# A delta-rule attention block with a quantised feed-forward: beta's products in four column groups of the TensorE array, and a new placing of NOPs in PE's stream

## The chip, the cores and the metric

The kernel runs on one core of a Trainium2 chip. Its engines are named as the profile names them: PE (TensorE, with PEld for its weight loads), DVE (VectorE), ACT (ScalarE), POOL (GpSimd) and SP (SyncE, which issues most DMAs). The metric is the time of one execution on the device in microseconds, the median of several runs.

## The reference

Input x has shape [2, 4096, 512]. With xn its layer norm, the output is x + attention(xn) + feed-forward(xn).

```python
q, k = xn @ Wq, xn @ Wk;  v = silu(xn @ Wv)         # 16 heads of 32
q, k = l2n(q) * 32 ** -0.5, l2n(k)                  # per head
beta = sigmoid(xn @ Wb)                             # one number per token and head
# per head, over the 4096 tokens:
#   S_t = S_{t-1} + k_t (beta_t * (v_t - S_{t-1}^T k_t))^T ;  o_t = S_t^T q_t
o = o * rsqrt(mean(o * o) + 1e-5) * o_norm_weight
attention = o @ Wo
feed_forward = ((silu(xn @ f8(gate) * gs) * (xn @ f8(up) * us)) @ f8(down)) * ds   # inner width 1536
```

Wb has 16 columns, one per head, where Wq, Wk and Wv have 512: beta is the smallest of the projections.

## The kernel before, in words

**Spans.** The 4096 tokens are cut into 16 spans of 256 tokens for each of the two batch rows, so a span has TOK = 512 tokens, held as TILES = 4 tiles of 128. All 16 spans are written out in Python (`all_spans`, `for turn in range(TURNS)`), each engine in its own stream with waits on semaphores. The first span is the opening, in which weights are still rounded and scaled. Precision comes from splitting: xn stands in SBUF as `xt_hi` and `xt_lo` (fp16, features on the partitions, 512 tokens along the row), the weights as `w_hi` and `w_lo`; a product of a projection is the sum of hi x hi, hi x lo and lo x hi over 4 slices of 128 features.

**PE in a span.** `project(job)` (L440) makes one block of 128 output columns for all 512 tokens, in 12 products of 128x512, into one of four PSUM banks D. The jobs in order are K0, Q0, K1, Q1, beta, (pair 0), K2, (pair 1), Q2, K3, (pair 2), Q3, first part of V0, (pair 3), the rest of V0 and V1 to V3. A pair, `grams_of(m)` (L465), is the key and query pair of head group m: 64 small fp32 products in tiles of 32x32, each of them two loads and two products in the profile, four tiles at a time (`quads`, L370). It waits for `kwide_ready` and `qwide_ready`, which ACT raises when K and Q of that group are out of PSUM. After the projections come the output projection of the span before (L391, 48 products), 18 "halves" of the gate and up projection (`gate_up`, L455, 8 products of 128x512 each), and then the solve and the chain: 4 groups of solve products and 8 chunk steps, in which PE and DVE alternate and the rest of the feed-forward (`fill`) lies between them.

**Beta before.** Beta is job 4. Its weights take 128 columns of `w_hi` (L120), of which for each of the four head groups 4 hold the high part, 4 the low part, and 24 are zeros. Eight products of 128x512 (L448 with two of the three parts) give D[bank] = [128, 512]. DVE's `b_to_tokens` (L1140) transposes all of it in blocks of 32x32 into `bt` (L1142) and adds high and low part into `tb` (L1147, three instructions, because the second batch row's heads are stored with the halves of the partitions exchanged, `parts_of`). ACT's `beta_tanh` (L684) is one activation on `tb` (L687). DVE's `beta_to_problems` then makes the sigmoid of it.

**DVE and ACT around it.** In every span after the opening DVE runs `prepare`: o_sums, k_to_tokens(0), k_to_tokens(1), o_scale, b_to_tokens, k_to_tokens(2), read_grams(0), mask_products(0), o_low, beta_to_problems and on to the solve, a chain of 62 instructions with others woven in (L1274, L1281). ACT runs evacuate_k(0), evacuate_q(0), evacuate_k(1), evacuate_q(1), evacuate_k(2), the high part of o (L717, released by DVE's o_scale), beta_tanh, evacuate_q(2), evacuate_k(3), evacuate_q(3). In the opening, ACT has squares and magnitudes of weights between the evacuations, with beta_tanh ahead of evacuate_k(2), and DVE does its k_to_tokens(0) to (3) in a row (L1133, twelve instructions).

**Slots.** PE's code arrives in blocks of 256 instructions. `addr_align(256, offset=s, max_nops=n)` pads with NOPs until the next instruction stands in slot s of its block. Before, each span after the opening has one such place, in the gate and up run behind half 8 (L514), with 14 NOPs each time; a span is then 18 blocks of instructions long.

## Time and profile before

| | us |
|---|---|
| median of 3 runs | 2225.53 (2224.4 to 2226.23) |
| the profiled execution | 2224.83 |
| its span in the profile | 2222.9 |
| PE busy | 2103.2 (95%) |
| DVE busy | 1874.2 (84%) |
| ACT busy | 1113.6 (50%) |
| POOL busy | 281.8 (13%) |

The busy time of PE counts a product until its modelled end, so products that follow each other closely overlap in it: a product of 128x512 has 0.38 us, and the next one starts about 0.22 us after it. Start times are therefore the better measure. The share of busy time is a mean over stages: in the chain PE and DVE wait for each other, elsewhere PE runs through.

### The profile page before, as it was taken

What the parts mean: (1) busy time and instruction counts of PE and PEld (TensorE: products, weight loads), DVE (VectorE), ACT (ScalarE), POOL (GpSimd) and SP (SyncE); (2) the same over time, 40 slices, a digit from 0 to 9 for tenths busy, and PEclk for the clock granted to TensorE, in tenths of its full rate; (3) what the DMA queues carried; (4) which work ended last, traced back from release to release, by engine and by line L of the source; (5) the groups of instructions that cost most, each with busy time, mean ns of one, the idle gap of its engine ahead of it and who ended that gap; (6) DMA issues with size and microseconds to landing.
All of it is one profiled execution on the core that took longest, in us unless ns stands there. A gap on an engine that the chain in (4) does not pass through costs nothing.

```text
span 2222.9 us, 82460 instructions
## 1 busy us (share of the span) xinstructions
PE 2103.2 (95%) x36464; PEld 1085.0 (49%) x36592; DVE 1874.2 (84%) x3381; ACT 1113.6 (50%) x2840; POOL 281.8 (13%) x534
## 2 busy tenths in 40 slices
PE   2889999999999999999999999999999999999996
PEld 1445454554445555454554545455454554545453
DVE  8988979888797888979888797888979888797886
ACT  4673644636355363644636355462644637355442
POOL 3101111020110201111020110201111020111100
PEclk9999999999999999999999999999999999999998
DMA  7001111001111001111001111001111001111000
GB/s 270 14 9 22 39 22 40 15 10 39 22 40 22 12 31 22 39 23 39 17 8 40 22 40 22 12 31 22 39 22 40 17 7 40 22 39 22 12 12 21
DMA packets 89953, 68.49 MB, mean 31 GB/s; under 512 B 68480, under 2 KB 68480, under 8 KB 89600
## 3 DMA queue, kind: packets, MB, share of 16 engines
q1 hardware_dynamic: 88880, 63.20, 9.7%
q8 instruction: 289, 4.73, 0.9%
q14 instruction: 64, 0.52, 0.1%
q10 hardware_dynamic: 720, 0.03, 0.0%
HBM read 30.72 MB, written 16.78 MB: 21 GB/s over the span
## 4 chain that ended last, share of the span: by engine, by line
PE 86%; DVE 6%; ACT 4%; issue 3%; DMA 1%; SPq 0%; ACTq 0%; DVEq 0%
PE D L460 27%; PE D L450 23%; PE D L525 13%; PE T L375 12%; PE D L391 8%; PE T L367 4%; DVE state L1388 2%; ACT kpv L752 1%; ACT at L777 1%; ACT f_hi L739 1%; DVE outer_p L1384 1%; DMA qt<-in_L_attn_Wq_dram 1%; DVE outer_v L1274 0%; DVE at L1281 0%; DVE amax L1003 0%
## 5 line engine op out<-in xcount | busy, mean ns | idle before, releaser
L460 PE MATMUL D<-xt,wgu 128*128 128x512 f16 x3072 | 685.8, 380 | 9.8 <-ACT sg L745 6.4
L450 PE MATMUL D<-xt,w_hi 128*128 128x512 f16 x1664 | 489.8, 381 | 24.1 <-DVE w_lo L1046 24.1
L460 PEld LDWEIGHTS D<-xt,wgu 128*128 128x128 f16 x3072 | 292.6, 98 | 360.2 <-ACT sg L745 6.9
L450 PE MATMUL D<-xt,w_lo 128*128 128x512 f16 x768 | 292.3, 381 | 0.0
L525 PE MATMUL D<-wd,f_lo 128*128 128x512 bf16 x704 | 267.3, 380 | 13.0 <-issue 12.0
L833 ACT ACTIVATE qt<-T 64x128 f32<-64x128 f32 (+1 forms) x384 | 104.7, 273 | 347.8 <-DVE outer_p L1384 344.8
L525 PE MATMUL D<-wd,f_hi 128*128 128x512 bf16 x704 | 267.3, 380 | 10.2 <-issue 10.2
L1274 DVE TENSOR_TENSOR outer_v<-mt,at 128x62 f32<-128x62 f32 (+15 forms) x496 | 260.6, 525 | 13.6
L1281 DVE TENSOR_TENSOR at<-at,outer_v 128x62 f32<-128x62 f32 (+15 forms) x496 | 260.3, 525 | 11.8
L450 PEld LDWEIGHTS D<-xt,w_hi 128*128 128x128 f16 x1664 | 159.1, 98 | 213.0 <-issue 26.9
L735 ACT ACTIVATE kpv<-kpv,rk 128x32 f32<-128x32 f32 x1024 | 231.1, 308 | 35.5 <-DVE kpv L1138 35.5
L745 ACT ACTIVATE sg<-D,gs 128x512 f32<-128x512 f32 x192 | 131.4, 685 | 185.1 <-PE D L460 184.2
L949 POOL TENSOR_TENSOR xs<-xs,fuse 128x512 f32<-128x512 f32 x64 | 81.1, 1267 | 777.8 <-DVE fuse L1357 777.8
L729 ACT ACTIVATE sg<-D,w_inv 64x256 f32<-64x256 f32 (+1 forms) x192 | 90.3, 470 | 108.2 <-PE D L450 106.6
L391 PE MATMUL D<-wo_hi,qt 128*128 128x512 f16 x480 | 142.8, 379 | 0.0
L1388 DVE SCALAR_TENSOR_TENSOR state<-outer_p,of_pair,state 128x256 f32<-128x256 f32 x256 | 125.5, 531 | 4.5
L450 PEld LDWEIGHTS D<-xt,w_lo 128*128 128x128 f16 x768 | 75.3, 98 | 91.0 <-issue 1.4
L375 PEld LDWEIGHTS T<-kpv 32*32 32x32 f32 x8192 | 89.9, 103 | 55.8 <-issue 55.0
L367 PEld LDWEIGHTS T<-kq,state 64*64 64x64 f32 x4096 | 76.8, 134 | 76.5 <-issue 76.4
L1296 DVE STREAM_TRANSPOSE kq<-T 128x256 f32<-128x256 f32 x128 | 56.9, 444 | 67.4 <-PE T L375 67.4
L525 PEld LDWEIGHTS D<-wd,f_hi 128*128 128x128 f16 x768 | 74.9, 98 | 75.9 <-issue 3.9
L367 PE MATMUL T<-kq,state 64*64 64x64 f32 x4096 | 92.8, 225 | 19.9 <-DVE state L1388 10.3
(181 smaller groups left out, 2864.5 us busy)
## 6 DMA issues: line engine op xcount, KB each, us to landing
xs<-_attn_hidden_states_dram SPq DMA_DIRECT2D x32, 512.0 KB, 3.4
out_dram<-xs SPq DMA_DIRECT2D x32, 512.0 KB, 2.8
fuse<-in_L_ffn_gate_w_dram SPq DMA_DIRECT2D x2, 768.0 KB, 8.9
xs<-in_L_ffn_up_w_dram SPq DMA_DIRECT2D x2, 768.0 KB, 9.0
f_hi<-in_L_ffn_down_w_dram SPq DMA_DIRECT2D x2, 768.0 KB, 10.5
f_lo<-in_L_ffn_down_w_dram SPq DMA_DIRECT2D x2, 768.0 KB, 12.0
kpv<-in_L_attn_Wk_dram SPq DMA_DIRECT2D x1, 1024.0 KB, 11.4
qt<-in_L_attn_Wq_dram SPq DMA_DIRECT2D x1, 1024.0 KB, 13.6
```

Of the source, the lines that this page charges most:

```text
L367: last = nc.tensor.matmul(out[to], lhs[s], rhs[s], start=True, stop=True)
L375: last = nc.tensor.matmul(out[to], lhs[s], rhs[s], start=True, stop=True)
L391: ins = nc.tensor.matmul(D[bank][:, :], o_part[:, m, j * P:(j + 1) * P], w[:, m, :], start=n == 0, stop=n == 11)
L450: last = nc.tensor.matmul(D[bank][:, :], w[:, k, cols], xp[:, k, :], start=n == 0, stop=n == len(products) - 1)
L460: last = nc.tensor.matmul(D[bank][:, :], wgu[:, n // 2, c:c + P], (xt_hi, xt_lo)[n % 2][:, n // 2, :], start=n == 0, stop=n == 2 * KT_ - 1)
L525: last = nc.tensor.matmul(D[bank][:, :], (f_hi, f_lo)[n % 2][:, ic, j * P:(j + 1) * P], wd[:, ic, :], start=n == 0, stop=n == 2 * IC - 1)
L735: return nc.scalar.activation(v_problem, v_problem, ACT.Identity, scale=rk[:, n:n + 1])
L745: nc.scalar.activation(sg[:, ic % 2, :], D[bank_of(gate_up_job(2 * ic))][:, :], ACT.Silu, scale=gs[:, ic:ic + 1]).then_inc(sg_ready, 1)
L833: last = nc.scalar.activation(ot_v[to, b, c], chain_banks(c)[src, b, :, 1, :], ACT.Copy)
L1274: solved[0] = step(nc.vector.tensor_tensor(products(j), m_prob[:, :, j, j + 1:].unsqueeze(3).to_broadcast(shape), t_prob[:, :, j, 0:j + 1] ...
L1281: solved[0] = step(nc.vector.tensor_tensor(rest, rest, products(j), ALU.subtract))
L1388: ins = nc.vector.scalar_tensor_tensor(half, outer_p[:, 0:256].rearrange("p (n d) -> p n d", d=DH), of_pair[:, e:e + 1], half, ALU.mult, A ...
```

## The change

Beta's weights now take 32 columns: 16 with the high parts and 16 with the low parts. PE computes beta in a function of its own, `project_beta`: for each of the 4 slices of features and each of `xt_hi` and `xt_lo` there are four products, one per tile of 128 tokens, with 32 weight columns and 128 moving columns; the four are placed in the column groups 0, 32, 64 and 96 of the array (`tile_position=(0, 32 * j)`) and write 32 partitions each of the same bank. It is called where job 4 stood, in front of pair 0. That makes 32 loads and 32 products out of 8 and 8. DVE transposes a block of 128x128 instead of 128x512 and adds high and low part in one instruction, in place, for all heads (`b_sum`, in `bt`). The change of layout that DVE's three adds made passes to ACT: tanh is now 16 activations, one for each of 4 tiles and 4 head groups, each from 32 partitions of `b_sum` to 32 partitions of `tb`. Because `bt` is also the target of sums whose result nobody reads, ACT's `sum_rows` gets a wait for `tb_ready`.

The NOPs change too: one alignment at the start of the opening, and one behind each of the 18 early halves of every span, spaced by a formula (`slot_after`). A span is then 19 blocks long, since beta adds 48 instructions and the NOPs are 222 instead of 14.

The diff, without the edit that drops the zeroing of the unused weight columns:

```diff
--- before.py
+++ after.py
@@ -71,7 +71,14 @@
     return job % 4 if job < JOB_DN + 3 else JOB_DN % 4
 
 
-FETCH_SLOTS, SPAN_SLOT, PADDING = 256, 249, 15
+FETCH_SLOTS, OPENING_SLOT, HALF_SLOT, FILLING = 256, 133, 94, 222
+
+
+def slot_after(half):
+
+    return (HALF_SLOT + 4 * KT_ * half + FILLING * (half + 1) // EARLY_HALVES) % FETCH_SLOTS
+
+
 FILL_UW, FILL_CHAIN = 10, (6, 7)
 
 
@@ -117,7 +124,7 @@
             return ctx.enter_context(nc.semaphore(name))
 
 
-        w_hi = sb("w_hi", [P, KT_, 3 * DM + P], F16)
+        w_hi = sb("w_hi", [P, KT_, 3 * DM + 2 * HEADS], F16)
         w_lo = sb("w_lo", [P, KT_, 3 * DM], F16)
         wo_hi = sb("wo_hi", [P, MS, DM], F16)
         wo_lo = sb("wo_lo", [P, MS, DM], F16)
@@ -197,6 +204,7 @@
         fused = [fuse[:, ic % 4, :] if ic // 4 != 1 else qt[:, :, :].rearrange("p n t -> p (n t)")[:, (ic - 4) * TOK:(ic - 3) * TOK] for ic in range(IC)]
         x_parts = mt[:, :].bitcast(F16).rearrange("p (j a d) -> p j a d", j=TILES, a=2)
         unused = bt[:, :, :].rearrange("p n t -> p (n t)")
+        b_sum = bt[:, 4:8, 0:HEADS]
         kq_flat = kq[:, :, :, :].rearrange("p n a t -> p (n a t)")
         o_wide = qt[:, :, :].rearrange("p n t -> p (n t)")
         o_half = o_wide.bitcast(F16)
@@ -441,9 +449,9 @@
                         if opening and not first:
                             pe.wait_ge(proj_ready, 2 if job == JOB_K[0] else 5 if job in JOB_V else 3)
                         bank = bank_of(job) if first else take(job)
-                        group = (4, 0, 5, 1, 12, 6, 2, 7, 3, 8, 9, 10, 11)[job]
+                        group = (4, 0, 5, 1, None, 6, 2, 7, 3, 8, 9, 10, 11)[job]
                         cols = slice(group * P, (group + 1) * P)
-                        parts = ((w_hi, xt_hi), (w_hi, xt_lo), (w_lo, xt_hi))[:2 if job == JOB_B else 3]
+                        parts = ((w_hi, xt_hi), (w_hi, xt_lo), (w_lo, xt_hi))
                         products = [(k, w, xp) for k in range(KT_) for w, xp in parts]
                         for n in range(first, min(end, len(products))):
                             k, w, xp = products[n]
@@ -451,6 +459,18 @@
                                                     start=n == 0, stop=n == len(products) - 1)
                         if n == len(products) - 1:
                             last.then_inc(dense_done, 1 + TILES if opening and job == JOB_V[MS - 1] else 1)
+
+                    def project_beta():
+
+                        if opening:
+                            pe.wait_ge(proj_ready, 3)
+                        bank = take(JOB_B)
+                        products = [(k, xp) for k in range(KT_) for xp in (xt_hi, xt_lo)]
+                        for n, (k, xp) in enumerate(products):
+                            for j in range(TILES):
+                                last = nc.tensor.matmul(D[bank][32 * j:32 * j + 32, 0:P], w_hi[:, k, 3 * DM:], xp[:, k, j * P:(j + 1) * P],
+                                                        start=n == 0, stop=n == len(products) - 1, tile_position=(0, 32 * j))
+                        last.then_inc(dense_done, 1)
 
                     def gate_up(half, first=0, end=2 * KT_):
                         bank = bank_of(gate_up_job(half)) if first else take(gate_up_job(half))
@@ -480,9 +500,12 @@
                         last.then_inc(tiled_done, 2)
 
 
+                    if opening:
+                        pe.addr_align(FETCH_SLOTS, offset=OPENING_SLOT, max_nops=FETCH_SLOTS - 1)
                     pe.wait_ge(*((xt_lo_ready, TILES) if opening else (xt_landed, since(16 * TILES))))
-                    for job in range(5):
+                    for job in range(4):
                         project(job)
+                    project_beta()
                     grams_of(0)
                     project(5)
                     grams_of(1)
@@ -510,8 +533,7 @@
                             project_out(j, take(JOB_WO[j]))
                     for half in range(EARLY_HALVES):
                         gate_up(half)
-                        if half == 8 and not opening:
-                            pe.addr_align(FETCH_SLOTS, offset=SPAN_SLOT, max_nops=PADDING)
+                        pe.addr_align(FETCH_SLOTS, offset=slot_after(half), max_nops=FETCH_SLOTS - 1)
 
                     def down(j, first, end):
 
@@ -684,7 +706,14 @@
                     def beta_tanh():
 
                         act.wait_ge(b_summed, since(1, 1))
-                        nc.scalar.activation(tb[:, :, :], tb[:, :, :], ACT.Tanh, scale=w_inv[:, 3:4]).then_inc(tb_ready, 1)
+                        for j in range(TILES):
+                            b, first = j // 2, STEPS * (j // 2) + 4 * (j % 2)
+                            src = slice(32 * j, 32 * j + 32)
+                            for h in range(QUADS):
+                                to = 32 * (h ^ 2 if b else h)
+                                last = nc.scalar.activation(tb[to:to + 32, :, first:first + 4], b_sum[src, :, MS * h:MS * h + MS].rearrange("p c m -> p m c"),
+                                                            ACT.Tanh, scale=w_inv[src, 3:4])
+                        last.then_inc(tb_ready, 1)
 
                     evacuate_k(0)
                     evacuate_q(0)
@@ -755,6 +784,7 @@
                     def sum_rows(j):
 
                         act.wait_ge(x_loaded[j // 2], since(16, 32))
+                        act.wait_ge(tb_ready, since(1, 1))
                         act.wait_ge(x_summed, since(TILES, j))
                         nc.scalar.activation(unused, xs[:, 1 - par, j, :], ACT.Copy, accum_out=x_sum[:, j:j + 1]).then_inc(x_summed, 1)
 
@@ -1033,12 +1062,12 @@
             one(nc.vector.tensor_tensor(k_least[:, :], k_least[:, :], k_least[:, :], ALU.mult))
             nc.vector.tensor_scalar(w_inv[:, 3:4], w_inv[:, 3:4], 0.5, None, ALU.mult).then_inc(scales_ready, 1)
 
-            wb_out = w_hi[:, :, 3 * DM:].rearrange("p k (h q) -> p k h q", q=32)
+            wb_out = w_hi[:, :, 3 * DM:].rearrange("p k (i h m) -> p k i h m", i=2, h=QUADS)
             wb_in = wb_raw[:, :, :].rearrange("p k (m h) -> p k h m", h=QUADS)
-            one(nc.vector.tensor_scalar(wb_out[:, :, :, 0:MS], wb_in, w_scale[:, 3:4], None, ALU.mult))
+            one(nc.vector.tensor_scalar(wb_out[:, :, 0], wb_in, w_scale[:, 3:4], None, ALU.mult))
             for k in range(KT_):
-                ins = nc.vector.scalar_tensor_tensor(wb_out[:, k, :, MS:2 * MS], wb_in[:, k], w_scale[:, 3:4],
-                                                     wb_out[:, k, :, 0:MS], ALU.mult, ALU.subtract)
+                ins = nc.vector.scalar_tensor_tensor(wb_out[:, k, 1], wb_in[:, k], w_scale[:, 3:4],
+                                                     wb_out[:, k, 0], ALU.mult, ALU.subtract)
             ins.then_inc(proj_ready, 1)
 
             def low_w(n, src):
@@ -1139,14 +1168,9 @@
 
                     def b_to_tokens():
                         bank = full(JOB_B)
-                        nc.vector.transpose(bt[:, :, :].rearrange("p c q -> p (c q)"), D[bank][:, :]).then_inc(b_raw, 1)
+                        nc.vector.transpose(bt[:, 0:4, :].rearrange("p c q -> p (c q)"), D[bank][:, 0:P]).then_inc(b_raw, 1)
                         dve.wait_ge(b_raw, since(1, 1))
-                        for b in range(BATCH):
-                            of_b = slice(b * STEPS, (b + 1) * STEPS)
-                            for to, src in parts_of(b):
-                                last = nc.vector.tensor_tensor(tb[to, :, of_b], bt[src, of_b, 0:MS].rearrange("p c m -> p m c"),
-                                                               bt[src, of_b, MS:2 * MS].rearrange("p c m -> p m c"), ALU.add)
-                        last.then_inc(b_summed, 1)
+                        nc.vector.tensor_tensor(b_sum, bt[:, 0:4, 0:HEADS], bt[:, 0:4, HEADS:], ALU.add).then_inc(b_summed, 1)
 
                     def beta_to_problems():
 
```

PE around beta in the span of turn 1 (`xt` against `w_hi` and `w_lo` are projections, `kq` is pair 0; one row of the pair is 64 products), before:

```order
L450 MATMUL D<-xt,w_hi 128x512 x2
L450 MATMUL D<-xt,w_lo 128x512
L450 MATMUL D<-xt,w_hi 128x512 x8
L375 MATMUL T<-kq 32x64 x64
L450 MATMUL D<-xt,w_hi 128x512 x2
```

and now:

```order
L458 MATMUL D<-xt,w_hi 128x512 x2
L458 MATMUL D<-xt,w_lo 128x512
L471 MATMUL D<-xt,w_hi 32x128 x32
L383 MATMUL T<-kq 32x64 x64
L458 MATMUL D<-xt,w_hi 128x512 x2
```

The eight wide products have become 32 narrow ones at the same place; nothing else moved here.

ACT in the same span, from the evacuation of K2 on (`kq` are evacuations, `qt` is the high part of o, `tb` is tanh), before:

```order
L668 ACTIVATE kq<-D 128x16x32
L717 ACTIVATE qt<-at 128x2048
L687 ACTIVATE tb<-tb,w_inv 128x64
L674 ACTIVATE kq<-D 128x16x32
L668 ACTIVATE kq<-D 128x16x32
L674 ACTIVATE kq<-D 128x16x32
```

and now:

```order
L690 ACTIVATE kq<-D 128x16x32
L746 ACTIVATE qt<-at 128x2048
L714 ACTIVATE tb<-bt,w_inv 32x4x4 x16
L696 ACTIVATE kq<-D 128x16x32
L690 ACTIVATE kq<-D 128x16x32
L696 ACTIVATE kq<-D 128x16x32
```

The order is the same; 16 small activations stand in front of evacuate_q(2), where one stood.

DVE in the same span, from the end of o_scale (`at`) to the read of the grams (`mt<-T`), before:

```order
L1099 SCALAR_TENSOR_TENSOR at<-qt,q_scale,mt 128x2048
L1142 STREAM_TRANSPOSE bt<-D 128x512
L1147 TENSOR_TENSOR tb<-bt 128x4x8
L1147 TENSOR_TENSOR tb<-bt 64x4x8 x2
L1133 STREAM_TRANSPOSE kpv<-kq 128x256
L1133 STREAM_TRANSPOSE kpv<-kq 64x256 x2
L1195 STREAM_TRANSPOSE mt<-T 128x1024
```

and now:

```order
L1128 SCALAR_TENSOR_TENSOR at<-qt,q_scale,mt 128x2048
L1171 STREAM_TRANSPOSE bt<-D 128x128
L1173 TENSOR_TENSOR bt<-bt 128x4x16
L1162 STREAM_TRANSPOSE kpv<-kq 128x256
L1162 STREAM_TRANSPOSE kpv<-kq 64x256 x2
L1219 STREAM_TRANSPOSE mt<-T 128x1024
```

Four instructions have become two, a smaller transpose and one add.

## Rows read from the trace of the kernel before

**Rows 1.** The page: span, busy time of each engine, one group of section 5.
```profile
span 2222.9 us, 82460 instructions
...
PE 2103.2 (95%) x36464; PEld 1085.0 (49%) x36592; DVE 1874.2 (84%) x3381; ACT 1113.6 (50%) x2840; POOL 281.8 (13%) x534
...
L450 PEld LDWEIGHTS D<-xt,w_hi 128*128 128x128 f16 x1664 | 159.1, 98 | 213.0 <-issue 26.9
```

**Rows 2.** Waits of PE from 200 to 2100 us: total, times, longest.
```profile
PE D L525 <- issue: 19.2, 108, 0.5
```

**Rows 3.** Timeline of PE, one span: start us, us, engine, operation, [idle before <-releaser].
```profile
1003.76 1.89 PE L450 MATMUL D<-xt,w_hi 128*128 128x512 f16 x8
1005.58 1.48 PE L375 MATMUL T<-kq 32*32 32x64 f32 x128
1006.99 0.60 PE L450 MATMUL D<-xt,w_hi 128*128 128x512 f16 x2
```

**Rows 4.** Timeline of PE, the first 0.17 us of that first pair.
```profile
1005.58 0.38 PE L375 MATMUL T<-kq 32*32 32x64 f32 x22
```

**Rows 5.** Timeline of ACT, the same span (the last row: a run of small activations).
```profile
1009.79 0.60 ACT L668 ACTIVATE kq<-D 128x512 f32<-128x512 f32 x1 [5.23 <-PE D L450]
1010.28 1.90 ACT L717 ACTIVATE qt<-at 128x2048 f16<-128x2048 f32 x1
1012.08 0.34 ACT L687 ACTIVATE tb<-tb,w_inv 128x64 f32<-128x64 f32 x1
1013.89 0.60 ACT L674 ACTIVATE kq<-D 128x512 f32<-128x512 f32 x1 [1.47 <-PE D L450]
1035.97 6.89 ACT L735 ACTIVATE kpv<-kpv,rk 128x32 f32<-128x32 f32 x32 [2.07 <-DVE kpv L1138]
```

**Rows 6.** Timeline of DVE, the same span.
```profile
1007.11 2.35 DVE L1099 SCALAR_TENSOR_TENSOR at<-qt,q_scale,mt 128x2048 f32<-128x2048 f32 x1
1009.38 0.71 DVE L1142 STREAM_TRANSPOSE bt<-D 128x512 f32<-128x512 f32 x1
1010.12 0.66 DVE L1147 TENSOR_TENSOR tb<-bt 128x32 f32<-128x32 f32 x3
1010.81 1.35 DVE L1133 STREAM_TRANSPOSE kpv<-kq 128x256 f32<-128x256 f32 x3
1014.48 2.27 DVE L1211 TENSOR_TENSOR qt<-at,qt 128x2048 f16<-128x2048 f32 x1
1016.67 0.18 DVE L1154 TENSOR_SCALAR beta<-tb 128x64 f32<-128x64 f32 x1
1023.08 1.25 DVE L1195 STREAM_TRANSPOSE mt<-T 128x1024 f32<-128x1024 f32 x1 [0.99 <-PE T L375]
```

**Rows 7.** Timeline of PE: third pair, gate and up run, first solve product.
```profile
1016.38 1.48 PE L375 MATMUL T<-kq 32*32 32x64 f32 x128
...
1042.62 31.24 PE L460 MATMUL D<-xt,wgu 128*128 128x512 f16 x144
1073.79 1.45 PE L375 MATMUL T<-kpv,mt 32*32 32x64 f32 x112
```

**Rows 8.** PE sequencer, two lines: durations min/median/max in ns, first and last start.
```profile
L514 PEldq NOP  x14: 13/13/13, 1054.3 to 1055.3; - x14
...
L553 PEldq EVENT_SEMAPHORE  x2: 51/1668/3285, 1069.9 to 1075.2; - x2
```

**Rows 9.** Timeline of the opening: ACT, DVE and PE.
```profile
64.65 0.34 ACT L687 ACTIVATE tb<-tb,w_inv 128x64 f32<-128x64 f32 x1
71.33 0.59 ACT L668 ACTIVATE kq<-D 128x512 f32<-128x512 f32 x1
...
68.25 5.48 DVE L1133 STREAM_TRANSPOSE kpv<-kq 128x256 f32<-128x256 f32 x12
...
105.74 3.56 PE L460 MATMUL D<-xt,wgu 128*128 128x512 f16 x8 [6.44 <-ACT sg L745]
139.93 2.06 PE L375 MATMUL T<-kpv,mt 32*32 32x64 f32 x128 [3.75 <-issue]
```

More of the change, by code:

```diff
@@ L1003, in largest @@
                 nc.vector.tensor_reduce(amax[:, n:n + 1], src, AX, ALU.max, apply_absolute_value=True).then_inc(amax_ready, 1)
-            one(nc.vector.memset(w_hi[:, :, 3 * DM:], 0.0))
             one(nc.vector.memset(state[:, :, :, :, :], 0.0))
```

## The prediction, made before the changed kernel had run

> **What bounds the kernel now.** I read the page first: PE is busy 95% of 2222.9 us, DVE 84% [rows 1]. Then PE's waits over the spans after the first: the largest entry is 19.2 us over 108 waits of half a microsecond at most [rows 2]. Between the chain steps PE runs without a pause, so what is taken out of PE's stream can shorten each span, as long as nothing else comes due first. That "as long as" is read from the timelines of one steady span (turn 7, 993 to 1126 us): PE [rows 3, 4, 7], ACT [rows 5], DVE [rows 6]. The reader is to see there how late each engine delivers to the next.
>
> **Beta on PE.** Before: 8 products of 512 columns. Eight take 1.89 us to the modelled end and one takes 0.38, so a new one starts every 0.216 us; the first pair's products start at 1005.58, 1.82 us after beta's first [rows 3]. That is 8 x 0.216 = 1.73 and 0.09 us of change-over. After: 32 products of 128 columns, four side by side. One of 128 columns is a quarter of 0.216, 0.054 us; four at once give 8 x 0.054 = 0.43 us. Can PE issue them so fast? The pair's first 22 small products start within 0.17 us, 8 ns each, against the 13.5 ns needed here [rows 4], and all 128 take 1.41 us, 11 ns each [rows 3]. Beta now stands between two kinds of tiles, one more change-over: 0.09 to 0.15 us by the same rows. Gain on PE: 1.73 - 0.43 - 0.12 - 0.05 for a queue that reaches the pair less full = 1.1 us a span.
>
> No product in this trace uses all 128 rows with a group of 32 columns, so the price is bounded from both sides. Below: 0.35 us, 32 at 11 ns. Above: all in series, each with its load: 32 x (0.054 + 98 ns / 4 = 0.025) [rows 1] = 2.5 us, 0.8 more than now. I take 0.43, since the pairs next to it show four tiles at once at full rate, their loads hidden.
>
> A rule speaks against the change. In the pair's burst four tiles get 22 products and loads in 0.17 us, so a load runs beside a product even in its own tile, every fourth instruction [rows 4]. The Trainium skill, "TensorE: Matmul & The Clock Gate", Part 3, says that a weight load overlaps products in flight only when its row group differs; beta's four tiles share all row groups. By that rule the sum for beta would be the 2.5 us above; the trace does not bear it out for tiles of 32 rows, and has no tile of 128 rows. The same page's "3x col" packing (2.38 times) points the other way.
>
> **DVE.** `b_to_tokens` was a transpose of 0.71 and three adds in 0.66; k_to_tokens follows 1.43 us after its start [rows 6]. Now the transpose has a quarter of the elements: 512 columns take 0.71, 256 take 0.45 (three in 1.35), so 128 about 0.31, and one add about 0.24. DVE is 0.8 us ahead from here. It stays ahead up to the read of the second grams (1023.08), where it already waits 0.99 us for PE: there DVE takes PE's gain, whatever it is, up to 1.8 us. After that DVE works through to the solve's end, just in time for PE: the sequencer's wait for the solved matrices ends at 1069.9 + 3.3 = 1073.2 [rows 8] and PE needs them at 1073.79 [rows 7]. Both move by the same amount, so nothing is lost there.
>
> **ACT.** One activation becomes 16, with 16 elements each in 32 partitions. The nearest row is the run of 32 activations of 32 columns in 6.89 us, 6.89 / 32 = 0.215 each; with half the elements I take 0.205 [rows 5]. 16 x 0.205 = 3.3 us, against 0.25 before: 3.05 more. Bounds: half of 0.215 each (1.7 us, and ACT is in nobody's way), and 0.34 each, the full duration of the old one (5.4 us). What is behind it: evacuate_q(2), which the third pair on PE waits for. ACT's part starts with `o_high` (L717), released by DVE at 1007.11 + 2.35 = 1009.46. Before, the evacuation of K2 held it to 1010.28; with PE 1.1 us ahead that is over by 1009.2, so `o_high` starts at 1009.5, its 1.80 us (1012.08 - 1010.28) end at 1011.3, the 16 at 1014.6, evacuate_q(2) at 1015.2. With 0.2 us for the semaphore and the restart (bounds 0 and the 0.6 between 1073.2 and 1073.79) the third pair starts at 1015.4. It stood at 1016.38 [rows 7], and PE by itself would be there at 1015.3. So ACT leaves 1.0 of the 1.1 us. DVE asks for tanh at 1016.67 - 0.8 = 1015.9, after it is ready: no stall.
>
> **NOPs.** In place of 14 in one spot, each span has 18 alignments with 12 or 13 each: 256 + 14 - 48 (beta's new instructions) = 222. They cost the sequencer 14 in about 1.05 us, 0.075 us each. PE hides that: they are issued at 1054.3, while the products in front of them run until 1042.62 + 72 x 0.216 = 1058.2, 3.9 us of lead, and the run of 144 products keeps its pace (31.24 us) [rows 7, 8]. Now a half needs 12.3 x 0.075 + 0.15 = 1.1 us of sequencer for 1.73 us of products: hidden, a lead of about 3 us remaining. Without that cover it would cost 17 us a span, which I exclude. The blocks of code change place; I allow 0.1 us a span.
>
> **The opening.** ACT and DVE set its pace: PE waits 6.44 us for ACT at 105.74 and 3.75 us at 139.93 [rows 9]. ACT is busy behind tanh (64.65) up to evacuate_k(3), 71.33 + 0.59 = 71.9, which moves by 3.05 to 75.0. DVE's twelve transposes (5.48 us) need it for the last three, started at 72.4 before and now at 75.0: 2.6 us later, and DVE has no idle time up to the solve's end in which to win it back. The first alignment of the opening's gate and up run, counted from the slots, is 159 NOPs: about 12 us. Halves 0 to 3 began at 105.74 - 6.44 - 4 x 1.73 = 92.4, the NOPs would end near 102 and half 3 near 107; half 4 is held by ACT to 105.74 + 2.6 = 108.3. Covered; if the clock falls to 1.2 GHz in that gap, up to 3 us are not. I take 2.6 us for the opening, bounds 0 and 6.
>
> **Sum.** 15 spans x (1.0 - 0.1) = 13.5 less, opening 2.6 more: -10.9 us on the profiled execution's 2224.8 us, 2213.9. The median of the runs is 0.7 above it: 2214.6; I say 2214.
>
> **Rivals.**
> 1. No packing: the 32 products run one after another at 0.054, loads hidden. 1.73 us as before, 0.1 of change-over: +1.5, opening +2.6, so 2230. For it: no such tile in the trace. Against: [rows 4]. 0.12.
> 2. ACT takes the place, and it ends slower. If one small activation takes p, evacuate_q(2) ends at 1011.3 + 16p + 0.6, and the third pair starts later than 1016.38 from p = 0.27 on. At 0.34 it is 1.1 us late, and DVE's beta with it: 15 x 1.1 + opening 5 = 2247. For it: 0.34 is what the old one shows. Against: the pitch of 0.215 in a long run [rows 5]. 0.06.
> 3. Loads and products of one tile in series, the upper bound of beta above: 15 x 0.9 + 2.6, 2242. For it: no tile of 128 rows and 32 columns in the trace. Against: loads hidden in the pairs [rows 4]. 0.05. This is what the Trainium skill's rule on row groups ("TensorE: Matmul & The Clock Gate", Part 3) would bring.
> 4. The gain is halved: the tiles overlap in part, or the third code block in a row comes late behind beta's 64 and the pair's 256 instructions. 15 x 0.45 less, 2.6 more: 2221.5. 0.12.
> 5. The change doesn't do what it says in time: PE's gain arrives, but a wait elsewhere in the span returns it all: 2225 to 2228. Against: the waits I followed. 0.03.
>
> **Numbers.** My case 0.62, 2209 to 2219; the rivals 0.38. A run of this kernel can tell about 0.2%, 4.5 us, from no change. Faster (below 2221): 0.62 and most of rival 4, 0.71. Same (to 2230): the rest of it, rival 5, most of rival 1: 0.15. Slower: 0.14. The range for 8 in 10: 2208 (1.1 us a span kept whole, 16.5, and no loss in the opening) to 2230.
>
> **What would show it.** Right: beta's 32 products within 0.6 us, in front of the first pair; the pair still 1.4 to 1.5 us; the 16 activations in 3.3 us; the third pair released by evacuate_q(2), with PE idle 0.1 to 0.3 us; the run of 144 products at 31.2 us; a steady span about 1 us shorter; the opening's first solve product 2 to 3 us later than 139.93. Wrong: starts of beta's products 54 ns apart or more, PE idle inside the gate and up run, DVE idle ahead of the second grams' read for longer than now, or small activations at 0.27 us and more.

## The result, and the profile after

| | us |
|---|---|
| before, median of 4 runs beside it | 2225.88 (2224.40 to 2227.67) |
| after, median of 4 runs | 2261.02 (2260.10 to 2262.81) |
| after / before | 1.016, 95% interval 1.0148 to 1.0173 |
| the profiled execution after, and its span | 2261.94, 2260.2 |
| its mean granted clock of TensorE | 0.983 (before 0.994) |

The change makes the kernel 35 us slower. I had said 2214, range 2208 to 2230.

The page of after, against [rows 1]: PE has 36976 products and as many loads, 24.5 us more of busy time in a span 37.3 us longer.

```profile
span 2260.2 us, 87086 instructions
...
PE 2127.7 (94%) x36976; PEld 1086.2 (48%) x36976; DVE 1858.7 (82%) x3348; ACT 1189.9 (53%) x3080; POOL 281.5 (12%) x534
```

The waits of PE from 200 to 2200 us (total, times, longest): [rows 2] had as its largest entry many short ones. Now 15 waits, one in each steady span, lead the list, all on the line of the pairs (L383):

```profile
PE T L383 <- issue: 31.1, 15, 2.3
PE T L375 <- DVE state L1412: 9.1, 28, 0.3
```

PE's timeline in the span of turn 1, which starts at 198.14. The rows answer to [rows 3] and [rows 7].

```profile
208.28 0.38 PE L458 MATMUL D<-xt,w_lo 128*128 128x512 f16 x1
208.59 0.63 PE L471 MATMUL D<-xt,w_hi 128*32 128x128 f16 x32
209.15 1.48 PE L383 MATMUL T<-kq 32*32 32x64 f32 x128
...
219.63 0.38 PE L458 MATMUL D<-xt,w_lo 128*128 128x512 f16 x1
222.03 1.63 PE L383 MATMUL T<-kq 32*32 32x64 f32 x128 [2.02 <-issue]
223.60 1.03 PE L458 MATMUL D<-xt,w_hi 128*128 128x512 f16 x2
...
228.82 1.48 PE L383 MATMUL T<-kq 32*32 32x64 f32 x128
...
249.88 31.24 PE L480 MATMUL D<-xt,wgu 128*128 128x512 f16 x144
```

Beta takes 0.56 us from its first product to the pair, and the first pair stands 11.01 us after the span's start, where it stood 12.18 us after it: PE gains 1.17 us. Then PE stands still for 2.02 us in front of the third pair, which comes 23.9 us after the start where it came at 22.98. ACT's timeline, to set beside [rows 5], shows what it waits for:

```profile
213.36 0.60 ACT L690 ACTIVATE kq<-D 128x512 f32<-128x512 f32 x1 [4.07 <-PE D L458]
214.24 1.91 ACT L746 ACTIVATE qt<-at 128x2048 f16<-128x2048 f32 x1 [0.28 <-DVE at L1128]
216.05 5.26 ACT L714 ACTIVATE tb<-bt,w_inv 32x16 f32<-32x16 f32 x16
221.34 0.60 ACT L696 ACTIVATE kq<-D 128x512 f32<-128x512 f32 x1
```

The 16 activations take 5.29 us from start to next start, 0.330 each. evacuate_q(2) (L696) ends at 221.94 and the pair starts 0.09 us later. DVE's timeline, against [rows 6]:

```profile
214.12 0.31 DVE L1171 STREAM_TRANSPOSE bt<-D 128x128 f32<-128x128 f32 x1
214.46 0.22 DVE L1173 TENSOR_TENSOR bt<-bt 128x64 f32<-128x64 f32 x1
214.61 1.34 DVE L1162 STREAM_TRANSPOSE kpv<-kq 128x256 f32<-128x256 f32 x3
...
221.35 1.16 DVE L1178 TENSOR_SCALAR beta<-tb 128x64 f32<-128x64 f32 x1 [0.81 <-ACT tb L714]
...
230.33 1.25 DVE L1219 STREAM_TRANSPOSE mt<-T 128x1024 f32<-128x1024 f32 x1 [4.04 <-PE T L383]
```

DVE's own cost fell as forecast. It waits 0.81 us for tanh, which costs nothing: for the second grams it then waits 4.04 us for PE's fourth pair, which is late with the third, where it waited 0.99.

**A second loss behind the first.** From the third pair to the fourth is 6.79 us in this span (222.03 to 228.82); before it was 5.18 (22.98 to 28.16 after the start). The windows view (stretch, length, PE busy and products, PEclk, DMA share, GB/s) shows why. The last row is the same stretch of the next span (it takes in the fourth pair as well):

```profile
212.50:216.50 4.00, 4.00 (x141) 1.00 0.02 4
219.90:222.00 2.10, 0.11 (x1) 1.00 0.00 0
222.00:223.60 1.60, 1.57 (x129) 0.86 0.00 0
223.60:228.80 5.20, 5.20 (x19) 0.71 0.01 3
359.10:364.30 5.20, 5.20 (x146) 1.00 0.02 6
```

The granted clock was full up to the end of the 2.1 us in which PE had one product in flight, and fell to its lower level, 1.2 GHz, in the 1.6 us behind them (a mean of 0.86 there). In 10 of the 15 steady spans the records hold 3.4 us at half clock behind this wait; before, in none. (Both kernels also have half clock in the opening and in the last 30 us.) Each such stretch costs 1.6 us: the fourth pair starts 30.4 to 31.0 after the span's start in those ten, 29.1 in the other five.

**The account of the 37.3 us** between the two spans, from start times. The opening is 4.3 us longer (turn 1 starts at 198.14, before at 193.80). The 14 periods from there to the last span are 29.2 us longer (1894.2 against 1865.1): 14 x 0.92 = 12.9 for the late third pair, 9 x 1.6 = 14.4 for the half clock, and 1.9 over. By start times those 1.9 lie behind the first solve product: from there to the next span it takes 52.96 us on the mean, before 52.82. With one tanh and the same slots (below) it is 53.03, so they come with the rest of the change, most likely with the new places of PE's code, and not with ACT. The last span with what follows is 3.8 longer, 2.8 of it in front of its fourth pair.

### The profile page after: what moved, and what is told of

Read it like the earlier page. It is cut to its first block, busy times and chain, and to the rows that moved or that the text cites. A ratio compares the mean times of both kernels' runs of the same rounds, so it can differ in the third digit from the quotient of the medians.

```text
span 2260.2 us, 87086 instructions
## 1 busy us (share of the span) xinstructions
PE 2127.7 (94%) x36976; PEld 1086.2 (48%) x36976; DVE 1858.7 (82%) x3348; ACT 1189.9 (53%) x3080; POOL 281.5 (12%) x534
## 4 chain that ended last, share of the span: by engine, by line
PE 84%; DVE 7%; ACT 4%; issue 3%; DMA 1%; SPq 0%; ACTq 0%
PE D L480 26%; PE D L458 22%; PE D L547 12%; PE T L383 12%; PE D L399 7%; PE T L375 4%; DVE state L1412 2%; ACT kpv L781 1%; ACT at L807 1%; ACT f_hi L768 1%; DVE outer_p L1408 1%; DVE kpv L1397 1%; DMA qt<-in_L_attn_Wq_dram 1%; DVE outer_v L1298 0%; DVE at L1305 0%
## 5 line engine op out<-in xcount | busy, mean ns | idle before, releaser
L458 PE MATMUL D<-xt,w_hi 128*128 128x512 f16 x1536 | 471.4, 389 | 24.4 <-DVE w_lo L1075 24.4
L458 PE MATMUL D<-xt,w_lo 128*128 128x512 f16 x768 | 297.7, 388 | 0.0
L547 PE MATMUL D<-wd,f_lo 128*128 128x512 bf16 x768 | 292.4, 381 | 0.0
L547 PE MATMUL D<-wd,f_hi 128*128 128x512 bf16 x768 | 292.1, 380 | 0.0
L458 PEld LDWEIGHTS D<-xt,w_hi 128*128 128x128 f16 x1536 | 148.9, 100 | 206.1 <-issue 41.6
L383 PE MATMUL T<-kq 32*32 32x64 f32 x8192 | 97.3, 229 | 36.3 <-issue 31.1
L383 PEld LDWEIGHTS T<-kpv 32*32 32x32 f32 x8192 | 90.6, 103 | 59.2 <-issue 58.1
L383 PEld LDWEIGHTS T<-kq 32*32 32x32 f32 x8192 | 86.7, 105 | 59.4 <-issue 57.7
L383 PE MATMUL T<-kpv 32*32 32x64 f32 x8192 | 111.9, 222 | 3.2 <-DVE kpv L1397 3.2
## 6 DMA issues: line engine op xcount, KB each, us to landing
f_hi<-in_L_ffn_down_w_dram SPq DMA_DIRECT2D x2, 768.0 KB, 10.1
```

What stands on the lines that cost most here:

```text
L383: last = nc.tensor.matmul(out[to], lhs[s], rhs[s], start=True, stop=True)
L458: last = nc.tensor.matmul(D[bank][:, :], w[:, k, cols], xp[:, k, :], start=n == 0, stop=n == len(products) - 1)
L547: last = nc.tensor.matmul(D[bank][:, :], (f_hi, f_lo)[n % 2][:, ic, j * P:(j + 1) * P], wd[:, ic, :], start=n == 0, stop=n == 2 * IC - 1)
```

## The experiments

Ratios are against the kernel before on the same chip, with 95% intervals.

**One tanh.** After, with the 16 activations replaced by one. It leaves out the change of layout, so most heads get another head's beta.

```diff
-                        for j in range(TILES):
...
-                                last = nc.scalar.activation(tb[to:to + 32, :, first:first + 4], b_sum[src, :, MS * h:MS * h + MS].rearrange("p c m -> p m c"),
-                                                            ACT.Tanh, scale=w_inv[src, 3:4])
+                        last = nc.scalar.activation(tb[:, :, :], b_sum[:, :, :], ACT.Tanh, scale=w_inv[:, 3:4])
```

> The changed kernel with one activation of 128x64 in place of the sixteen; it leaves out that beta's heads move between partitions, so beta is a wrong one for most heads. Beta's packing on PE, DVE's two instructions and all NOPs stay. Theory A (the sixteen activations hold evacuate_q(2), PE stands idle in front of the third pair, and its clock falls after that idle time in 10 of 15 spans): the third pair starts 21.8 us after the span's start, no stretch at half clock in the steady spans, 1.0 to 1.2 us less than before in each span: 2207 to 2213 us. Rival B (the 222 NOPs, or the narrow products and their change-over, cost the time): stays above 2240.

Measured: 2207.89, before 2225.01, ratio 0.9921 (0.9905 to 0.9938). The third pair starts 21.81 us after the span's start in each steady span, 1.17 ahead of before; no half clock follows it; PE's waits have no entry above the short ones:

```profile
PE D L547 <- issue: 15.7, 99, 0.2
```

So the 16 activations cost 53 us, more than the whole loss, and the rest of the change gains 17. This alone doesn't tell their duration from their number or their place.

**The sixteen in the kernel before.** Before, with 16 such activations ahead of its own tanh, results into a tile that nobody reads. `sum_rows` gets the wait of the change.

```diff
+        tb_small = sb("tb_small", [P, MS, BC])
...
+                        for j in range(TILES):
...
+                                nc.scalar.activation(tb_small[to:to + 32, :, first:first + 4], bt[src, 0:4, MS * h:MS * h + MS].rearrange("p c m -> p m c"),
+                                                     ACT.Tanh, scale=w_inv[src, 3:4])
                         nc.scalar.activation(tb[:, :, :], tb[:, :, :], ACT.Tanh, scale=w_inv[:, 3:4]).then_inc(tb_ready, 1)
```

> The kernel before with sixteen small activations added in front of the one tanh; their results go to a tile of their own. Nothing on PE or DVE changes. Theory A: the third pair moves from 22.98 to about 24.7 us after the span's start (16 x 0.33 = 5.3 us more on ACT, of which 1.9 were free before and 1.7 fall on PE), so 15 x 1.75 = 26 us, some 5 us in the opening, and 0 to 16 us from half clock: 2257 to 2273. Rival B: near 2226.

Measured: 2262.93, ratio 1.0166 (1.0149 to 1.0183). The third pair stands at 24.88 where it stood at 22.98, and PE waits for it in each span:

```profile
PE T L376 <- issue: 27.5, 15, 1.8
```

The 16 hold the third pair back without the rest of the change too, but what they cost is not the same: 38 us here, 53 there. The half clock came in only 2 of 15 spans here, behind waits of 1.8 us; after had it in 10, behind 2.02 us or a little more. 15 x 1.9 us, 8.6 us in the opening and 3.3 for the two stretches at half clock make 40.4, against 39.6 between the two profiled executions.

**The NOPs alone.** Before, with after's alignments (270 NOPs a span, which makes 19 blocks without beta's 48).

```diff
-FETCH_SLOTS, SPAN_SLOT, PADDING = 256, 249, 15
+FETCH_SLOTS, OPENING_SLOT, HALF_SLOT, FILLING = 256, 133, 94, 270
...
-                        if half == 8 and not opening:
-                            pe.addr_align(FETCH_SLOTS, offset=SPAN_SLOT, max_nops=PADDING)
+                        pe.addr_align(FETCH_SLOTS, offset=slot_after(half), max_nops=FETCH_SLOTS - 1)
```

> The kernel before with the alignments of the changed one (18 a span and one in the opening, 270 NOPs a span so that a span is 19 blocks). Theory A: the NOPs are hidden behind PE's products, and the other places of the code blocks give or take 0.2 us a span: 2223 to 2230. Rival B: a good part of the 35 us, 2240 and more.

Measured: 2219.46, ratio 0.9975 (0.9966 to 0.9985). 256 more NOPs a span cost nothing, and the new places even bring 0.25%: 5.5 us, where I had allowed a gain of 0.2 us a span at most. The 14 periods sum to 1859.6 against 1865.1, 0.39 us a period, all of it behind the first solve product. The waits that stood in [rows 2] shrink too:

```profile
PE D L533 <- issue: 15.6, 98, 0.2
```

**Forms of the small activation.** After, with another form in each span (two spans a form), so beta is another in most.

```diff
+        wide = sb("wide", [P, MS, 64])
...
+                        form = turn % 8
...
+                            elif form == 2:
+                                last = nc.scalar.activation(tb[to:to + 32, :, first:first + 4], b_sum[src, :, MS * h:MS * h + MS].rearrange("p c m -> p m c"), ACT.Tanh, scale=0.5)
+                            elif form == 3:
+                                last = nc.scalar.activation(wide[:, :, 4 * n:4 * n + 4], b_sum[:, :, MS * h:MS * h + MS].rearrange("p c m -> p m c"), ACT.Tanh, scale=w_inv[:, 3:4])
+                            elif form == 4:
+                                last = nc.scalar.activation(wide[src, :, 4 * n:4 * n + 4], b_sum[src, :, MS * h:MS * h + MS].rearrange("p c m -> p m c"), ACT.Tanh, scale=w_inv[src, 3:4])
...
```

> The changed kernel with another form of the sixteen activations in each span, turn modulo 8: 0 as it is; 1 Identity for Tanh; 2 a constant for the scale; 3 all 128 partitions; 4 same partitions in and out; 5 sixteen elements in a row; 6 all 128 partitions and in a row; 7 as 6 with Identity. Beta is wrong in most of them. It asks why one takes 0.330 us from start to start and not the 0.215 of the long run of 128x32. If the fewer partitions do it, 3, 6 and 7 are at 0.215 and the rest at 0.33; if Tanh does it, 1 and 7 are at 0.215; if the move between partitions does it, 4 joins them; if the stepped access does it, 5, 6 and 7. I hold the number of partitions for the likeliest.

Measured (one run, 2230.19). Groups of ACT by line: busy us, mean ns of one, then idle before. For L717, L723 and L725 the 32 durations sum to 10.1, 9.8 and 9.8, but the busy time counts what overlaps once:

```profile
L717 ACT ACTIVATE tb<-bt,w_inv 32x16 f32<-32x16 f32 x32 | 10.1, 316 | 0.4
L727 ACT ACTIVATE wide<-bt,w_inv 32x16 f32<-32x16 f32 x32 | 9.7, 303 | 0.4
L725 ACT ACTIVATE wide<-bt,w_inv 32x16 f32<-32x16 f32 x32 | 7.5, 305 | 0.1
L721 ACT ACTIVATE tb<-bt 32x16 f32<-32x16 f32 x32 | 7.2, 226 | 0.3
L723 ACT ACTIVATE wide<-bt,w_inv 128x16 f32<-128x16 f32 x32 | 7.0, 306 | 0.0
```

| form | us from one start to the next |
|---|---|
| as in after (L717); the same with Identity | 0.329; 0.329 |
| sixteen elements in a row, other partitions (L727) | 0.316 |
| constant scale, other partitions (L721) | 0.237 |
| same 32 partitions in and out (L725), mean | 0.234 |
| of these: inside a four on the same 32; from one four to the next | 0.214; 0.316 |
| all 128 partitions in and out (L723) | 0.212 |
| 128 partitions, in a row; with Identity | 0.198; 0.198 |

With a scale from SBUF each lasts about 0.3 us in every form. What differs is the overlap, and L725 shows on what it depends. There four activations in a row use the same 32 partitions, the next four the next 32, and so on. Four take 0.94 us, and the fifth, the first on other partitions, adds 0.33:

```profile
617.57 0.94 ACT L725 ACTIVATE wide<-bt,w_inv 32x16 f32<-32x16 f32 x4
617.57 1.27 ACT L725 ACTIVATE wide<-bt,w_inv 32x16 f32<-32x16 f32 x5
```

An activation starts 0.09 us before the last has ended if it writes the partitions that the last one wrote. If it writes others there is no overlap, and the full duration counts. It isn't the way from an activation's input to its own output that counts: in after, four of the 16 keep their partitions, and the step behind them is 0.316 to 0.334 us in every steady span, as behind the others, because the next one writes elsewhere. The input stays on the same 32 partitions there for four in a row, so a change of the output alone is enough; no run kept the output and changed the input, and none put the 16 in an order that writes the same partitions several times in a row. The number of partitions, which I had named as the likeliest reason, is none (0.214 against 0.212). A scale read from SBUF makes the moving form 0.09 longer, sixteen elements in a row make it 0.013 shorter, and the function doesn't matter.

**One tanh, other slots.** The first experiment with other positions of the alignments (with the same beta as there).

```diff
-FETCH_SLOTS, OPENING_SLOT, HALF_SLOT, FILLING = 256, 133, 94, 222
+FETCH_SLOTS, OPENING_SLOT, HALF_SLOT, FILLING = 256, 181, 142, 222
```

> As the kernel with one activation of 128x64 (beta wrong for most heads), with both slots 48 further on (OPENING_SLOT 181, HALF_SLOT 142), which puts the 256 borders of PE's code in the chain where the kernel of before with the alignments alone had them. If the borders inside the state products cost what the traces suggest (52.97 us against 52.39 from the first solve product to the next span), it is 0.5 us a span faster: 2199 to 2202. If they don't matter, 2208.

Measured: 2201.30, ratio 0.9892 (0.9875 to 0.9908); 6.6 us less for two numbers. From the first solve product to the next span it takes 52.4 us, where it took 53.0.

**A constant scale.** After with the new slots, DVE multiplies by the scale and the 16 activations have none from SBUF. It computes all of the reference.

```diff
-                                                            ACT.Tanh, scale=w_inv[src, 3:4])
+                                                            ACT.Tanh)
...
-                        nc.vector.tensor_tensor(b_sum, bt[:, 0:4, 0:HEADS], bt[:, 0:4, HEADS:], ALU.add).then_inc(b_summed, 1)
+                        nc.vector.tensor_tensor(b_sum, bt[:, 0:4, 0:HEADS], bt[:, 0:4, HEADS:], ALU.add).then_inc(b_raw2, 1)
+                        dve.wait_ge(b_raw2, since(1, 1))
+                        nc.vector.tensor_scalar(b_sum, b_sum, w_inv[:, 3:4], None, ALU.mult).then_inc(b_summed, 1)
```

> Full computation. The sixteen activations stay where they are, with a constant for the scale (one is 0.237 us from start to start then, by the kernel of forms); VectorE applies the scale in one more instruction of about 0.2 us; slots 48 further on. Theory A: evacuate_q(2) is 1.5 us earlier than in the changed kernel, the third pair starts 22.4 to 22.6 us after the span's start (21.81 without the activations, 23.9 with them at 0.33), no half clock in the steady spans: 0.4 a span less than before and 0.5 by the slots, opening 2.5 us more: 2212 to 2218. Rival: if not the start of evacuate_q(2) but something else in the sixteen counts, it stays above 2240.

Measured: 2214.57, ratio 0.9949 (0.9932 to 0.9966). The third pair comes at 22.41, PE's waits there are short, and no half clock follows them:

```profile
PE T L383 <- issue: 8.9, 15, 0.8
```

**Tanh behind evacuate_q(2).** After, in the spans behind the opening one line lower. It computes all of the reference.

```diff
-                        beta_tanh()
                         evacuate_q(2)
+                        beta_tanh()
```

> The changed kernel with the sixteen activations behind evacuate_q(2) instead of in front of it, in all spans but the opening. Theory A: the third pair starts at 21.8 us, PE doesn't idle there and no half clock follows, but now VectorE waits for beta: ready at 25.2 us after the span's start where it asks at 22.4, and it comes to its second read of the grams at 29.5 to 30.2, against 29.7 in the kernel before. The span is then set by VectorE: 2222 to 2238, most of the 35 us gone. If the sixteen cost PE their time in some other way than by evacuate_q(2), it stays above 2250.

Measured: 2212.71, ratio 0.9943 (0.9926 to 0.9959), better than I expected. The third pair starts at 21.81, when PE gets to it by itself. DVE now waits for beta, 2.71 us:

```profile
219.25 2.27 DVE L1235 TENSOR_TENSOR qt<-at,qt 128x2048 f16<-128x2048 f32 x1
224.24 0.20 DVE L1178 TENSOR_SCALAR beta<-tb 128x64 f32<-128x64 f32 x1 [2.71 <-ACT tb L714]
...
228.11 1.24 DVE L1219 STREAM_TRANSPOSE mt<-T 128x1024 f32<-128x1024 f32 x1
```

It reads the second grams (L1219) without a wait for PE, some 0.5 us behind the end of the fourth pair, and the first solve product stays 79.23 us after the span's start, as in the first experiment. Of the 2.71 us, 0.78 take the place of the wait that DVE has at the second grams with one tanh, and 1.45 come back in a small instruction (`kk_t`) that lasts 1.65 us with one tanh, beside a memset of POOL, and 0.20 here (see the last section). Most of the rest goes into a wait further on, in the gate and up run, where DVE waited for PE in the kernel before (first row) and no longer does (second row, again 75.9 us after the span's start, as with one tanh):

```profile
1070.45 0.75 DVE L1267 SCALAR_TENSOR_TENSOR qt<-D,usf,sg 128x512 f32<-128x512 f32 x1 [0.27 <-PE D L460]
```

```profile
275.00 0.75 DVE L1291 SCALAR_TENSOR_TENSOR qt<-D,usf,sg 128x512 f32<-128x512 f32 x1
```

The opening still has its tanh in the old place and turn 1 starts at 199.12, 5.5 us later than with one tanh.

**GpSimd moves, ACT has one tanh.** The full computation: 16 copies on POOL do the change of layout, tanh is one activation behind evacuate_q(2) (in the opening behind evacuate_k(2)), with the new slots.

```diff
+                    def move_beta():
...
+                                last = nc.gpsimd.tensor_copy(tb[to:to + 32, :, first:first + 4], b_sum[src, :, MS * h:MS * h + MS].rearrange("p c m -> p m c"))
...
-                        beta_tanh()
                         evacuate_q(2)
+                        beta_tanh()
```

> Full computation. GpSimd, which waits for VectorE at that time, moves beta's sums between the partitions in sixteen small copies, ScalarE keeps one tanh of 128x64, now behind evacuate_q(2) (in the opening behind evacuate_k(2)); slots 48 further on. If a copy takes up to 0.33 us, beta is ready when VectorE asks for it, and the packing's gain stays: 2200 to 2206. If a copy takes 0.5 us or slows VectorE at the port they share, beta comes 3 us late at VectorE, of which 1.8 are free: 2215 to 2225.

Measured: 2201.37, ratio 0.9890 (0.9873 to 0.9906), faster than both kernels and equal to the version with one tanh and no moves. On POOL a copy takes 0.36 us, longer than on ACT, but nobody waits in line behind them; DVE's wait is 0.48 us and the second grams are read with a wait for PE again:

```profile
209.56 5.78 POOL L951 COPY tb<-bt 32x16 f32<-32x16 f32 x16 [5.35 <-DVE bt L1181]
```

```profile
215.75 1.59 DVE L1186 TENSOR_SCALAR beta<-tb 128x64 f32<-128x64 f32 x1 [0.48 <-ACT tb L709]
...
221.37 1.25 DVE L1227 STREAM_TRANSPOSE mt<-T 128x1024 f32<-128x1024 f32 x1 [0.25 <-PE T L383]
```

**All NOPs in one place.** One tanh and the new slots, with all 222 NOPs of a span behind half 8.

```diff
-                        pe.addr_align(FETCH_SLOTS, offset=slot_after(half), max_nops=FETCH_SLOTS - 1)
+                        if opening or half == 8:
+                            pe.addr_align(FETCH_SLOTS, offset=(slot_after(17) - (16 * 9 if half == 8 else 0)) % FETCH_SLOTS if not opening else slot_after(half), max_nops=FETCH_SLOTS - 1)
```

> The kernel with one activation and slots 48 further on (beta wrong for most heads), with all 222 NOPs of a span behind half 8, not spread over 18 halves. At 0.075 us each they hold PE's sequencer for 16.7 us, and PE has 3.9 us of products in its queue: 12.8 us of idle time a span and 1.7 us or more at half clock, 15 x 14.5 more: near 2420. If NOPs were nearly free, 2201.

Measured (one run): 2425.3. PE stands still for 12.2 us in each span, inside the gate and up run:

```profile
240.88 15.70 PE L480 MATMUL D<-xt,wgu 128*128 128x512 f16 x72
268.81 17.55 PE L480 MATMUL D<-xt,wgu 128*128 128x512 f16 x72 [12.23 <-issue]
```

The second 72 take 1.85 us longer. The clock is at half for 13.7 us of each span, most of it inside the wait, and the rest meets these products. So the NOPs are free only because they are spread: 12 or 13 behind each half stay within the lead of PE's queue, 222 at once exceed it.

## Why the prediction was wrong, step by step

**The step that failed: ACT, "with half the elements I take 0.205".** The sum used 16 x 0.205 = 3.3 us; it was 16 x 0.330 = 5.29. Everything behind it on the way to the third pair was right: with my own times and 0.33 each, evacuate_q(2) ends at 1011.3 + 5.3 + 0.6 = 1017.2, and the third pair comes 0.8 to 1.0 us later than 1016.38; 0.92 was measured. Rival 2 had this mechanism, the threshold of 0.27 and the case 0.34, and I gave it 0.06. The fault lies in the row I took the time from. [Rows 5] has 0.215 for activations that all write the same 128 partitions, where the next one overlaps the last; the changed ones write other partitions each time. The trace of before had such activations, and I didn't read them: V's evacuation writes all partitions, then one half, then the other (`parts_of`), and its three activations of 0.47 us each take 1.44, so they don't overlap. An activation that writes all 128, also out of PSUM, is overlapped by 0.11 us when the next writes all 128 too:

```profile
1024.69 1.44 ACT L729 ACTIVATE sg<-D,w_inv 128x256 f32<-128x256 f32 x3 [3.51 <-PE D L450]
...
1044.55 0.69 ACT L745 ACTIVATE sg<-D,gs 128x512 f32<-128x512 f32 x1 [1.69 <-PE D L460]
1045.13 0.95 ACT L735 ACTIVATE kpv<-kpv,rk 128x32 f32<-128x32 f32 x4
```

At the least, 0.215 and 0.34 should have stood beside each other with like weight. The duration of the old tanh, 0.34, was a better guide than the pitch of the long run.

**The term that was missing: the clock.** I allowed for half clock only in the opening. PE's 2 us in front of the third pair brought it in 10 steady spans, 16 us in all, as much as the lateness itself (15 x 0.92 = 14). Rival 2 therefore ended at 2247 and not at 2261. In the runs half clock came behind none of the waits of up to 0.8 us in front of the third pair, behind 2 of the 15 of 1.8 us (the kernel before with the sixteen), behind 10 of the 15 of about 2.0 us (after), and in every span that had a wait of 12.2 us. Why it comes in some spans and not in others with the same wait stays open.

**Beta on PE: right.** 32 products stand 13.3 ns apart, 0.43 us, and 0.56 to the pair; the gain is 1.17 us against 1.1. Rivals 1 and 3 fell. The rule of the Trainium skill ("TensorE: Matmul & The Clock Gate", Part 3) that a load overlaps only products in another row group isn't borne out: these four tiles share all 128 rows, and their loads are hidden. The ordinary products of the kernel before had shown it already: they use all rows, have loads of 98 ns [rows 1] and start 0.216 us apart [rows 3], where a load in front of each product would make it about 0.31.

**DVE: right** in its durations, 0.31 and 0.22 us against 0.31 and 0.24. That DVE finds tanh ready fell with the ACT term, without cost. That DVE works through from the second grams to the solve was too strict: it waits for PE once more in the gate and up run, and with tanh late by 2.71 us the first solve product did not move.

**NOPs: right.** The run of 144 products has its 31.24 us, and the experiments with all NOPs alone and with all in one place show both the cover and what it is worth. The 0.1 us a span for the blocks of code had the right size (0.14 behind the first solve product), but I had not seen it as something to win: two other slot numbers brought 6.6 us.

**The opening: right in direction.** 4.3 us against 2.6. evacuate_k(3) ends at 75.26 + 0.59, 3.93 later than in [rows 9]: 16 x 0.330 - 0.24 = 5.0 more, less the 1.1 by which tanh starts earlier, at 63.52, which my 3.05 had left out. The first solve product comes 3.45 later, and 0.9 more is lost from there to turn 1. The halves, though, were not held by ACT at half 4 as I wrote: the first half started at 96.04, and PE then stood still for the first alignment's NOPs. That this time was lost anyway is argued, not isolated: from 122.66 on PE waits for DVE as it did before from 119.22 on, and in the kernel before the same kind of alignments left the opening as long as it was (turn 1 at 193.65, against 193.80).

```profile
96.04 1.89 PE L480 MATMUL D<-xt,wgu 128*128 128x512 f16 x8
105.74 16.39 PE L480 MATMUL D<-xt,wgu 128*128 128x512 f16 x64 [7.81 <-issue]
...
143.38 1.71 PE L383 MATMUL T<-kpv,mt 32*32 32x64 f32 x128 [3.75 <-issue]
```

**The sum, put right.** The profiled execution's 2224.8 with 15 x (0.92 + 0.1), 10 x 1.6 and 4.3 gives 2260.4; measured 2261.9.

## What to carry to other kernels

A change of layout that is taken from one engine must be paid on another, and in an ordered stream it is paid in front of whatever stands behind it there. Price a small instruction by a row that has its operands and its neighbours, the partitions that one and the next write above all, and where none has, forecast with the duration, not with the pitch of a run. And where a wait of some microseconds arises on PE, look at the granted clock behind it: the same again can be lost there.

## What the runs showed of the hardware that I had not expected

- ACT: an activation of 16 elements in 32 partitions with a scale from SBUF lasts 0.29 to 0.32 us. The next one starts 0.21 us after it if it writes the same partitions, and 0.316 to 0.330, without overlap, if it writes others. A constant scale takes 0.09 us from the latter.
- PE: in tiles of 128 rows and 32 columns, four column groups side by side, products of 128 columns start 13.3 ns apart on the mean, with a load each.
- PE: where the NOPs put the later code is worth 0.4 to 0.6 us a span here (52.8 to 52.4 us and 53.0 to 52.4 us from the first solve product to the next span). That the borders of the code blocks are the reason is what I chose the slots by; no run separates it from other effects of the place, or one border from another.
- POOL and DVE: DVE's beta, 0.18 us in [rows 6], took 1.16 us in after and 1.59 in the version with the moves. In both it began while POOL's memset of 1.80 us ran, and ended 0.05 us behind it (the POOL rows below, of after and of the version with the moves, end at 222.45 and 217.28). The kernel before has the same loss one place on: there `kk_t`, 0.20 us elsewhere, takes 1.65 and ends 0.04 us behind the memset (first rows). In 150 steady spans, all but those of tanh behind evacuate_q(2), one of the two small instructions is stretched so. There the memset runs while DVE waits for tanh, and they take 0.20 and 0.21 us in all 15 spans. A transpose of 0.25 us in between isn't stretched. What the engines share here no run shows, and none moved the memset by itself.

```profile
1016.87 1.80 POOL L925 MEMSET at<- 128x2048 f32 x1 [12.14 <-DVE qt L1211]
```

```profile
1017.06 1.65 DVE L1161 TENSOR_SCALAR kk_t<-mt,k_least 128x32 f32<-128x32 f32 x1
```

```profile
220.65 1.80 POOL L955 MEMSET at<- 128x2048 f32 x1 [11.18 <-DVE qt L1235]
```

```profile
215.48 1.80 POOL L963 MEMSET at<- 128x2048 f32 x1
```
